# Twelve of the 32 depthwise chunks tap by tap on VectorE, nine rounds of convs on TensorE, the last one the 3x3 conv alone beside the batch norm's chain

## The chip, the cores and the metric

One core of a Trainium2 chip. The time is that of one execution on the device, in microseconds (us); that of a kernel is the median of its runs.

## What is computed

The input x is (8, 32, 64, 64) in float32. A bidirectional LSTM with 16 hidden units runs over the rows, a linear layer brings it back to 32 channels, and with x as a residual it goes into a second block. That block is what the change touches:

```python
def offset_branch(x, dw_w, dw_b, bn_g, bn_b, pw_w, pw_b):
    h = conv2d(x, dw_w, dw_b, padding=1, groups=x.shape[1])   # depthwise 3x3
    h = jax.nn.relu(batchnorm(h, bn_g, bn_b))
    return conv2d(h, pw_w, pw_b, padding=0)                   # 9 offsets a pixel
```

It is computed twice, with the weights of the x and of the y offsets. Beside it stands a full 3x3 conv of the same image from 32 to 32 channels (in the kernel it is already multiplied by the weights that fuse the branches). The offsets then shift the image along x and along y with linear interpolation, both results are projected, and the three are fused, normalized over the batch, passed through ReLU and added to the block's input.

## The kernel before, in words

**Layout.** The 8 images lie as 4 quadrants of 32 channels (128 partitions) by 2 halves `b` of 4096 pixels. All of it is cut into `NCH` = 16 chunks of 8 image rows, 512 pixels (`CH`); chunks 0 to 7 are half 0, chunks 8 to 15 half 1. `pad` is the image with a border of one pixel, 66 x 66. `h_x` and `h_y` take the results of the two depthwise convs (called hx and hy below), `acc` that of the 3x3 conv. `h_y` is stored transposed: within a half, the column index is the slow one (`hyt`, `hy_chunk`).

**Order.** Every engine has its own program, written out by hand; they meet at semaphores. There is no scheduler. An engine does its instructions in the order in which they are written, and one that waits holds all behind it.

**The conv stage** (line 898 on TensorE). Three kinds of jobs, `j` = 0 the 3x3 conv, 1 hx, 2 hy, with 16 chunks each: 48 jobs. Each job is nine taps of four matmuls, one for every quadrant, of 32 x 32 weights over 512 pixels in float32, accumulated in one PSUM bank. Four jobs make a round, and for each tap the matmuls of the four follow one another, so that the 16 positions of 32 x 32 in the array are all in use: quadrant q of job i writes to quadrant (q + i) % 4 of its bank. That makes 12 rounds, on banks 0 to 3 and 4 to 7 in turn (`conv_bank`). A round begins when the banks of the round before last have been read.

A job whose place i is not the usual place of its kind (`PLACES`) lands with its quadrants turned. The conv must be turned back to the image's order; hx and hy can stay turned, if the offset matmuls know the place (`X_PLACE`, `PLACES[2]`).

**Evacuation.** ScalarE (line 466) reads conv and hy banks and adds the bias; a turned bank costs four instructions of 32 partitions in place of one. VectorE (line 670) does that for hx, and takes `bn_stats` of each hx and hy chunk (lines 675 and 679).

**The batch norm's chain** (`norm`, lines 529 to 559). When the last statistics are there VectorE aggregates them, TensorE averages the means over the quadrants (line 786) and then the variances (line 788), ScalarE takes the root (line 401), and VectorE makes scale and shift.

**Offsets.** In four rounds `rd` of four chunks: VectorE (lines 688 and 689) and ScalarE (line 482) apply scale, shift and ReLU to a quarter (2048 elements a partition) of `h_x` and `h_y`; TensorE makes the offsets of x in banks 0 to 3 and of y in banks 4 to 7 (line 921); ScalarE (line 490) and VectorE (line 696) write them in bf16 parts, with masking matmuls between (line 929). After that comes the long loop of the sampling, which is not changed.

**Names the change touches**: `norm_mm` on TensorE, `norm_sqrt`, `relu_y_round` and `parts_x` on ScalarE, `CONV_ROUNDS`, `conv_bank`, `X_PLACE`, `vecs` (a table with one column a vector, loaded at the start).

## Time and profile before

| | us |
|---|---|
| median of 3 runs | 845.68 |
| lowest and highest | 842.84, 846.45 |
| the profiled execution | 846.11 |
| its span, first to last instruction | 844.2 |
| TensorE busy | 729.8 (86%) |
| VectorE busy | 612.0 (73%) |
| ScalarE busy | 492.6 (58%) |
| GpSimd busy | 259.6 (31%) |

All times of the trace count from the span's start. PE is TensorE, PEld its weight loads, DVE VectorE, ACT ScalarE, POOL GpSimd. A float32 matmul leaves two records. An instruction's duration includes its start and its drain, so the next one on the same engine can begin a little before its end. Convs, the norm's chain and offsets lie between 235 and 407 us.

### The profile page before, as it was taken

To read this page: it belongs to the slowest core of one execution; us is meant where nothing else is said; L and a number is where in the kernel's file an instruction comes from. 1 tells how busy PE (TensorE), PEld (TensorE's weight loads), DVE (VectorE), ACT (ScalarE), POOL (GpSimd) and SP (SyncE) were. 2 spreads that over 40 slices of the span, in tenths; PEclk is the share of its full clock that TensorE was granted. 3 is DMA by queue.
4 is the path that set the end of the run, shared out by engine and by line. 5 is a ranking of instruction groups with operands and counts; after the bars stand their busy time and mean duration, and the time that the engine had idled before them with its cause. 6 is when DMAs were issued, how large, how long until landed. Compare 5 with 4: busy or idle time off the path is not lost.

```text
span 844.2 us, 61069 instructions
## 1 busy us (share of the span) xinstructions
PE 729.8 (86%) x27570; PEld 590.9 (70%) x27570; DVE 612.0 (73%) x1126; ACT 492.6 (58%) x1008; POOL 259.6 (31%) x284
## 2 busy tenths in 40 slices
PE   0589999999689999587779999999999999999970
PEld 0355555557258899432469999999989999999960
DVE  4466666665812322568758999999999999999975
ACT  0344444443332432366658888878878887888854
POOL 1122222210000000000224445454465656656533
PEclk9999999999879999789999999999999999999995
DMA  9200000000000000000000000000000000000006
GB/s 238 89 2 2 0 0 0 0 2 1 4 3 4 5 4 4 4 1 1 3 4 0 0 0 0 0 0 0 0 0 0 0 0 0 0 0 0 0 2 199
DMA packets 4062, 12.04 MB, mean 14 GB/s; under 512 B 1391, under 2 KB 1787, under 8 KB 3460
## 3 DMA queue, kind: packets, MB, share of 16 engines
q1 hardware_dynamic: 1716, 4.88, 2.1%
q10 hardware_dynamic: 1522, 4.21, 1.8%
q0 software_dynamic: 768, 2.10, 0.9%
q8 instruction: 48, 0.79, 0.4%
q14 instruction: 8, 0.07, 0.0%
HBM read 6.99 MB, written 4.19 MB: 13 GB/s over the span
## 4 chain that ended last, share of the span: by engine, by line
PE 66%; DVE 17%; ACT 8%; issue 5%; DMA 2%; POOL 2%; ACTq 0%; DVEq 0%; POOLq 0%
PE psum L1022 17%; PE psum L951 16%; PE psum L898 13%; PE psum L977 8%; PE psum L969 5%; DVE wide L608 5%; DVE wide L611 4%; ACT wide L423 4%; ACT wide L419 3%; PE psum L921 2%; DVE offs L696 2%; DMA xs<-in_x_dram 2%; DVE stats L643 1%; POOL out_dram L254 1%; DVE xs L652 1%
## 5 line engine op out<-in xcount | busy, mean ns | idle before, releaser
L509 ACT ACTIVATE wide<-psum 128x512 f32<-128x512 f32 x576 | 301.5, 600 | 15.1 <-PE psum L951 8.1
L951 PE MATMUL psum<-wide,sels 125*32 125x256 bf16 x4608 | 231.9, 275 | 3.1 <-issue 2.5
L1022 PE MATMUL psum<-wide 128*32 128x64 f32 x8192 | 194.9, 220 | 3.4 <-issue 3.4
L720 DVE TENSOR_SCALAR wide<-wide 128x1024 f32<-128x1024 f32 x256 | 180.2, 724 | 2.8 <-ACT wide L509 2.6
L1022 PEld LDWEIGHTS psum<-wide 128*32 128x32 f32 x8192 | 169.6, 110 | 5.2 <-issue 3.9
L727 DVE COPY wide<-psum 128x1024 f32<-128x1024 f32 x128 | 156.1, 1219 | 2.0
L359 POOL COPY wide<-offs 125x256 bf16 (+1 forms) x64 | 28.7, 449 | 389.3 <-DVE offs L696 212.7
L351 POOL TENSOR_SCALAR wide<-wide 128x512 f32<-128x512 f32 x64 | 135.9, 2123 | 7.2 <-ACT wide L509 7.2
L898 PE MATMUL psum<-img,offs 32*32 32x512 f32 x3456 | 112.3, 610 | 5.8 <-ACT img L451 5.8
L977 PE MATMUL psum<-wc,wide 32*64 32x128 f32 x4096 | 112.7, 283 | 1.3 <-issue 1.3
L816 PEld LDWEIGHTS psum<-wide 128*64 128x64 f32 x2048 | 70.3, 137 | 61.0 <-DVE wide L619 60.0
L898 PEld LDWEIGHTS psum<-img,offs 32*32 32x32 f32 x3456 | 95.8, 104 | 21.5 <-issue 8.7
L951 PEld LDWEIGHTS psum<-wide,sels 125*32 125x32 bf16 x4608 | 91.1, 97 | 21.3 <-issue 13.7
L816 PE MATMUL psum<-wide 128*64 128x64 f32 x2048 | 87.2, 228 | 15.0 <-DVE wide L619 13.6
L969 PEld LDWEIGHTS psum<-wc,wide 32*64 32x64 f32 x2048 | 82.0, 133 | 18.3 <-issue 18.1
L969 PE MATMUL psum<-wc,wide 32*64 32x32 f32 x2048 | 89.4, 218 | 4.4 <-POOL wide L364 2.6
L977 PEld LDWEIGHTS psum<-wc,wide 32*64 32x64 f32 x4096 | 91.8, 132 | 1.5 <-issue 1.5
L423 ACT ACTIVATE wide<-wide 128x64 f32<-128x64 f32 x128 | 32.8, 256 | 93.8 <-DVE wide L611 93.8
L804 PE MATMUL psum<-wide 128*64 128x256 f32 x512 | 78.4, 388 | 0.0
L670 DVE TENSOR_SCALAR wide<-psum,vecs 128x512 f32<-128x512 f32 x16 | 11.6, 749 | 76.1 <-PE psum L898 76.1
L619 DVE SCALAR_TENSOR_TENSOR wide<-wide 128x64 f32<-128x64 f32 x128 | 33.2, 259 | 42.3 <-ACT wide L423 42.3
L505 ACT ACTIVATE y<-psum 64x256 f32<-64x256 f32 x64 | 24.2, 379 | 67.5 <-PE psum L969 67.5
(101 smaller groups left out, 772.8 us busy)
## 6 DMA issues: line engine op xcount, KB each, us to landing
xs<-in_x_dram ACTq DMA_DIRECT2D x8, 256.0 KB, 10.7
xs<-in_x_dram SPq DMA_DIRECT2D x8, 256.0 KB, 10.1
out_dram<-wide SPq DMA_DIRECT2D x16, 128.0 KB, 3.5
out_dram<-wide POOLq DMA_DIRECT2D x16, 128.0 KB, 4.2
offs<-in_cw_dram ACTq DMA_DIRECT2D x1, 576.0 KB
sels<-in_sel_dram ACTq DMA_DIRECT2D x1, 562.5 KB
wide<-in_dsc_dram ACTq DMA_DIRECT2D x1, 288.0 KB
offs<-in_dwd_dram ACTq DMA_DIRECT2D x1, 288.0 KB
```

The source lines that it names most:

```text
L351: nc.gpsimd.tensor_scalar(v8[:, par], v8[:, par], 1.0, 1.0, ALU.min, ALU.subtract).then_inc(v8_ready, 1)
L423: nc.scalar.activation(tc_[:, b], cells[:, b, 4, :], ACT.Tanh, scale=0.5).then_inc(tc_ready[b], 1)
L509: nc.scalar.activation(hat_tile(par, i), use_bank(par, hat_use(i)).rearrange("p (q n) -> p q n", q=2), ACT.Abs).then_inc(d_read, 1)
L720: nc.vector.tensor_scalar(v, v, 1.0, 1.0, ALU.min, ALU.subtract).then_inc(v_ready, 1)
L727: nc.vector.tensor_copy(yt[:, par, q:q + 2], psum[:, Y_BANK[q] * CH:(Y_BANK[q] + 2) * CH].rearrange("p (q r m) -> p q r m", q=2, r=HROWS)) ...
L804: last = mm(bank[DQ * d:DQ * d + DQ, (g % 2) * GROUP * S:(g % 2 + 1) * GROUP * S], wx_s[:, d, g, :], xst[:, par, d, :, b * S:(b + 1) * S], ...
L816: last = mm(gates[half, g], whh_s[:, g, half], hst[:, (j - 1) % UNROLL, b * S:(b + 1) * S], start=False, stop=True, skip_group_check=True)
L898: last = mm(conv_bank(m, i)[C * to:C * to + C, :], w, pad[rows, b, r0 + t // 3:r0 + t // 3 + ROWS, t % 3:t % 3 + S], start=(t == 0), stop= ...
L951: last = mm(bank[c, e * SL:(e + 1) * SL], sels[:, k, c], oc[0:NROW, par, :], start=(e == 0), stop=(e == 1))
L969: last = mm(use_bank(par, Y8_USE)[S * e:S * e + S, at:at + C], xc[c, par, r8 * S:(r8 + 1) * S], wcv[c, 0, 8, :], start=(r8 == 0 and tiles ...
L977: last = mm(ps[Y_BANK[q]][S * e:S * e + S, r * P:(r + 1) * P], xc[c, par, r * S:(r + 1) * S], wcv[c, 0, e:8:2, :], start=(r == 0), stop=(r ...
L1022: last = mm(ps[O_BANK][C * q:C * q + C, cols], w, v, start=(group == 0), stop=(group == GROUPS - 1))
```

## The change

**What it does.** VectorE makes twelve depthwise chunks itself, in three blocks of four (`ON_DVE`): hy 0 to 3, hy 4 to 7, hx 0 to 3, all of image half 0. A block of 2048 pixels is nine passes: the first tap times its weight plus the bias (block 0 on VectorE, blocks 1 and 2 on ScalarE), then eight `scalar_tensor_tensor`, each of which multiplies a shifted view of the padded image by a tap's weight and adds it to the block in place. The source of the hy blocks is a transposed view (`rearrange("p h w -> p w h")`). The weights come as 18 new columns of `vecs`. Each block is followed by its own statistics and those of some of TensorE's rounds.

TensorE keeps 36 jobs, nine rounds: eight with both kinds, and a ninth, `CONV_ONLY`, with four chunks of the 3x3 conv. Ahead of its eighth tap stands the matmul of the norm's means, behind it that of the variances; the offset matmuls of round 0 wait for the ninth round's banks one by one.

ScalarE evacuates all of TensorE's banks, hx too. Depthwise chunks always stay turned and cost one instruction; a conv chunk at place 2 costs two of 64 partitions, at places 1 and 3 four of 32. The ninth round's banks are evacuated after the root, after the first ReLU, and between the first two writings of offsets.

The diff, without the lines for constants, semaphores and the weights' layout, and without the split of `norm_mm` into `norm_mean` and `norm_var` (the same two matmuls with the same waits):

```diff
--- before.py
+++ after.py
...
@@ -213,18 +214,36 @@
 
 
 
-        PLACES = {0: 0, 2: 1, 1: 2}
-        TURN = (0, 2, 1)
-        CONV_ROUNDS, made = [], [0, 0, 0]
-        for m in range(3 * NCH // 4):
-            kinds = (0, 2, 1, TURN[m % 3])
-            CONV_ROUNDS.append([])
-            for j in kinds:
-                CONV_ROUNDS[m].append((j, made[j]))
-                made[j] += 1
-        X_PLACE = {n: i for jobs in CONV_ROUNDS for i, (j, n) in enumerate(jobs) if j == 1}
-        def conv_bank(m, i):
-            return ps[4 * (m % 2) + i]
+
+        ON_DVE = ((2, 0), (2, 4), (1, 0))
+        DW_CHUNKS = 4
+        def conv_rounds():
+            conv, hy = iter(range(NCH)), iter(range(NCH // 2, NCH))
+            hx = iter(range(DW_CHUNKS, NCH))
+            rounds = []
+            for m in range(8):
+                rounds.append([(0, 0, next(conv)), (1, 2, next(hy)),
+                               (2, 0, next(conv)) if m % 2 else (2, 1, next(hx)), (3, 1, next(hx))])
+            rounds.append([(i, 0, next(conv)) for i in (0, 2, 1, 3)])
+            return rounds
+        CONV_ROUNDS = conv_rounds()
+        CONV_ONLY = len(CONV_ROUNDS) - 1
+
+        JOB_NO, X_PLACE, Y_PLACE = {}, {n: 0 for n in range(DW_CHUNKS)}, (0, 1)
+        for jobs in CONV_ROUNDS:
+            for i, j, n in jobs:
+                JOB_NO[j, n] = sum(1 for key in JOB_NO if key[0] == j) + 1
+                if j == 1:
+                    X_PLACE[n] = i
+        def conv_bank(m, k):
+            return ps[4 * (m % 2) + k]
+        def dw_block(j, n):
+
+            r0, rows = n * ROWS, DW_CHUNKS * ROWS
+            def src(t):
+                v = pad[:, 0, r0 + t // 3:r0 + t // 3 + rows, t % 3:t % 3 + S]
+                return v if j == 1 else v.rearrange("p h w -> p w h")
+            return src, hxv[:, 0, r0:r0 + rows, :] if j == 1 else hyt[:, 0, :, r0:r0 + rows]
         ROUNDS = 4
         RC = NCH // ROUNDS
 
...
@@ -450,31 +469,38 @@
             act.wait_ge(pad_zero, 2)
             nc.scalar.activation(pad[:, 1, 1:1 + S, 1:1 + S], xv[:, 1], ACT.Identity, bias=coef[:, GN2, 1, 1:2],
                                  scale=coef[:, GN2, 0, 1:2]).then_inc(pad_ready[1], 1)
-            for m, jobs in enumerate(CONV_ROUNDS):
-                for i, (j, n) in enumerate(jobs):
...
-                    act.wait_ge(made_by, n + 1)
-                    if i == PLACES[j]:
-                        last = evacuate(slice(0, P), slice(0, P))
+
+            act.wait_ge(pad_ready[0], 1)
+            for j, n in ON_DVE[1:]:
+                src, to = dw_block(j, n)
+                nc.scalar.activation(to, src(0), ACT.Identity, bias=vecs[:, V_DWB + j - 1:V_DWB + j],
+                                     scale=vecs[:, V_DWW + (j - 1) * K:V_DWW + (j - 1) * K + 1]).then_inc(dw_first, 1)
+
+            def evacuate(m, k):
+                i, j, n = CONV_ROUNDS[m][k]
+                made_by, done = ((conv_mm, conv_ev), (hx_mm, hx_ev), (hy_mm, hy_ev))[j]
+                bias = cbias if j == 0 else vecs[:, V_DWB + j - 1:V_DWB + j]
+                act.wait_ge(made_by, JOB_NO[j, n])
+
+                turns = 0 if j else i
+                for own, at in {0: ((slice(0, P), slice(0, P)),),
+                                2: ((slice(0, S), slice(S, P)), (slice(S, P), slice(0, S)))}.get(
+                                    turns, [(slice(C * q, C * q + C), slice(C * ((q + turns) % Q), C * ((q + turns) % Q) + C))
+                                            for q in range(Q)]):
+                    src = conv_bank(m, k)[at, :]
+                    if j == 2:
+                        to, src = hy_chunk(n, own), src.rearrange("p (h w) -> p w h", h=ROWS)
                     else:
-
-                        for q in range(Q):
-                            at, own = C * ((q + i) % Q), C * ((q + PLACES[j]) % Q)
-                            last = evacuate(slice(own, own + C), slice(at, at + C))
-                    last.then_inc(done, 1)
+                        to = (acc, h_x)[j][own, n * CH:(n + 1) * CH]
+                    last = nc.scalar.activation(to, src, ACT.Identity, bias=bias[at, 0:1])
+                last.then_inc(done, 1)
+
+            for m in range(CONV_ONLY):
+                for k in range(4):
+                    evacuate(m, k)
             norm_sqrt(BN, 2)
+            for k in range(2):
+                evacuate(CONV_ONLY, k)
 
             def relu_y_round(rd):
 
@@ -490,11 +516,14 @@
                         nc.scalar.activation(ob[0][0:ONE_ROW + 1, (RC * rd + 2 * n) * CH:(RC * rd + 2 * n + 2) * CH],
                                              psum[0:ONE_ROW + 1, 2 * n * CH:(2 * n + 2) * CH], ACT.Identity,
                                              bias=vecs[0:ONE_ROW + 1, V_PWB:V_PWB + 1]).then_inc(done, 1)
+                        if rd == 0 and done is part1[0] and n == 0:
+                            evacuate(CONV_ONLY, 3)
                     if done is part1[0] and rd + 1 < ROUNDS:
                         relu_y_round(rd + 1)
 
             act.wait_ge(norm_done, BN + 1)
             relu_y_round(0)
+            evacuate(CONV_ONLY, 2)
             for rd in range(ROUNDS):
                 parts_x(rd)
 
@@ -662,21 +691,32 @@
             nc.vector.tensor_scalar(pad[:, 0, 1:1 + S, 1:1 + S], xv[:, 0], coef[:, GN2, 0, 0:1],
                                     coef[:, GN2, 1, 0:1], ALU.mult, ALU.add).then_inc(pad_ready[0], 1)
 
-            for m, jobs in enumerate(CONV_ROUNDS):
-                for i, (j, n) in enumerate(jobs):
-                    if j == 1:
-                        v = h_x[:, n * CH:(n + 1) * CH]
-                        dve.wait_ge(hx_mm, n + 1)
-                        nc.vector.tensor_scalar(v, conv_bank(m, i)[:, :], vecs[:, V_DWB:V_DWB + 1], None, ALU.add
-                                                ).then_inc(hx_ev, 1)
-                for j, n in jobs:
-                    if j == 2:
-                        dve.wait_ge(hy_ev, n + 1)
-                        last = nc.vector.bn_stats(stats_hy[:, n, :], hy_chunk(n))
-                for j, n in jobs:
-                    if j == 1:
-                        dve.wait_ge(hx_ev, n + 1)
-                        last = nc.vector.bn_stats(stats[:, n, :], h_x[:, n * CH:(n + 1) * CH])
+            def dw_stats(j, n):
+                if j == 1:
+                    return nc.vector.bn_stats(stats[:, n, :], h_x[:, n * CH:(n + 1) * CH])
+                return nc.vector.bn_stats(stats_hy[:, n, :], hy_chunk(n))
+
+            def round_stats(m):
+                for i, j, n in CONV_ROUNDS[m]:
+                    if j:
+                        dve.wait_ge((hx_ev, hy_ev)[j - 1], JOB_NO[j, n])
+                        last = dw_stats(j, n)
+                return last
+
+            for k, (j, n) in enumerate(ON_DVE):
+                src, to = dw_block(j, n)
+                weight = lambda t: vecs[:, V_DWW + (j - 1) * K + t:V_DWW + (j - 1) * K + t + 1]
+                if k == 0:
+                    dve.wait_ge(pad_ready[0], 1)
+                    step(nc.vector.tensor_scalar(to, src(0), weight(0), vecs[:, V_DWB + j - 1:V_DWB + j], ALU.mult, ALU.add))
+                else:
+                    dve.wait_ge(dw_first, k)
+                for t in range(1, K):
+                    step(nc.vector.scalar_tensor_tensor(to, src(t), weight(t), to, ALU.mult, ALU.add))
+                for c in range(DW_CHUNKS):
+                    dw_stats(j, n + c)
+                for m in ((0, 1), (2, 3, 4), (5, 6, 7))[k]:
+                    last = round_stats(m)
             step(last)
             nc.vector.bn_aggr(mv[:, 0, :], stats[:, :, :])
             step(nc.vector.bn_aggr(mv[:, 1, :], stats_hy))
...
@@ -884,25 +933,26 @@
             read = [0, 0, 0]
             for m, jobs in enumerate(CONV_ROUNDS):
                 if m >= 2:
-                    for j, n in CONV_ROUNDS[m - 2]:
-                        read[j] = n + 1
+                    for i, j, n in CONV_ROUNDS[m - 2]:
+                        read[j] = JOB_NO[j, n]
                     pe.wait_ge(conv_ev, read[0])
                     pe.wait_ge(hx_ev, read[1])
                     pe.wait_ge(hy_ev, read[2])
                 for t in range(K):
-                    for i, (j, n) in enumerate(jobs):
+                    if m == CONV_ONLY and t == K - 2:
+                        norm_mean(BN, 2)
+                    for k, (i, j, n) in enumerate(jobs):
                         b, r0 = n // (NCH // 2), n % (NCH // 2) * ROWS
                         for q in range(Q):
                             rows, to = slice(C * q, C * q + C), (q + i) % Q
                             w = cwf[rows, t, rows] if j == 0 else dwd_s[rows, j - 1, t, :]
-                            last = mm(conv_bank(m, i)[C * to:C * to + C, :], w,
+                            last = mm(conv_bank(m, k)[C * to:C * to + C, :], w,
                                       pad[rows, b, r0 + t // 3:r0 + t // 3 + ROWS, t % 3:t % 3 + S],
                                       start=(t == 0), stop=(t == K - 1))
                         if t == K - 1:
                             last.then_inc((conv_mm, hx_mm, hy_mm)[j], 1)
-            norm_mm(BN, 2)
-
-            pe.wait_ge(conv_ev, NCH)
+            norm_var(BN, 2)
+
             pe.wait_ge(dmask_in, 16)
             for rd in range(ROUNDS):
                 b, n0 = rd // 2, rd % 2 * RC
@@ -912,10 +962,13 @@
                     if rd > 0 and n % 2 == 0:
                         for a in range(2):
                             pe.wait_ge(part3[a], 2 * rd - 2 + n // 2 + 1)
+                    if rd == 0 and n != 1:
+
+                        pe.wait_ge(conv_ev, NCH - 2 + max(n - 1, 0))
                     r0 = slice((n0 + n) * ROWS, (n0 + n + 1) * ROWS)
                     for a in range(2):
                         for q in range(Q):
-                            at = (q + (X_PLACE[b * NCH // 2 + n0 + n] if a == 0 else PLACES[2])) % Q
+                            at = (q + (X_PLACE[b * NCH // 2 + n0 + n] if a == 0 else Y_PLACE[b])) % Q
                             rows = slice(C * at, C * at + C)
                             rhs = (hxv if a == 0 else hyt)[rows, b, r0, :]
                             last = mm(ps[RC * a + n][C * q:C * q + C, :], pws[rows, a, :], rhs, start=True, stop=True)
```

**VectorE, between the padding of image half 0 and the batch norm's aggregation.** Before, its first rounds (`wide` holds hx and hy, `img` the padded image):

```order
L662 TENSOR_SCALAR img<-xs,small 128x64x64 [waits pad_zero,norm_done]
L670 TENSOR_SCALAR wide<-psum,vecs 128x512 [waits hx_mm]
L675 BN_STATS offs<-wide 128x6 [waits hy_ev]
L679 BN_STATS stats<-wide 128x6 [waits hx_ev]
L670 TENSOR_SCALAR wide<-psum,vecs 128x512 [waits hx_mm]
L675 BN_STATS offs<-wide 128x6 [waits hy_ev] x2
L679 BN_STATS stats<-wide 128x6 [waits hx_ev]
L670 TENSOR_SCALAR wide<-psum,vecs 128x512 [waits hx_mm] x2
L675 BN_STATS offs<-wide 128x6 [waits hy_ev]
```

Now, its first block, two rounds' statistics and the second block:

```order
L691 TENSOR_SCALAR img<-xs,small 128x64x64 [waits pad_zero,norm_done]
L711 TENSOR_SCALAR wide<-img,vecs 128x64x32 [waits pad_ready0]
L715 SCALAR_TENSOR_TENSOR wide<-img,vecs,wide 128x64x32 [waits link] x8
L697 BN_STATS offs<-wide 128x6 [waits link]
L697 BN_STATS offs<-wide 128x6 x3
L697 BN_STATS offs<-wide 128x6 [waits hy_ev]
L696 BN_STATS stats<-wide 128x6 [waits hx_ev] x2
L697 BN_STATS offs<-wide 128x6 [waits hy_ev]
L696 BN_STATS stats<-wide 128x6 [waits hx_ev]
L715 SCALAR_TENSOR_TENSOR wide<-img,vecs,wide 128x64x32 [waits dw_first]
L715 SCALAR_TENSOR_TENSOR wide<-img,vecs,wide 128x64x32 [waits link] x7
```

The evacuations of hx (line 670) are gone. In front of the first statistics stand nine operations over 2048 elements that wait for nothing of TensorE's.

**TensorE, from its last rounds of convs to the first masking matmul.** Before:

```order
L898 MATMUL psum<-img,offs 32x512 [waits hy_ev,hx_ev,conv_ev]
L898 MATMUL psum<-img,offs 32x512 x143
L786 MATMUL psum<-small,avgs 128x2 [waits mean_in]
L788 MATMUL psum<-small,avgs 128x2 [waits dev_in]
L921 MATMUL psum<-wide,pws 32x512 [waits relu_x,relu_y,dmask_in,conv_ev]
L921 MATMUL psum<-wide,pws 32x512 x31
L929 MATMUL psum<-offs,seq 124x512 [waits part1x]
L929 MATMUL psum<-offs,seq 124x512 [waits part1y]
```

Now:

```order
L949 MATMUL psum<-img,offs 32x512 [waits hy_ev,hx_ev,conv_ev]
L949 MATMUL psum<-img,offs 32x512 x111
L825 MATMUL psum<-small,avgs 128x2 [waits mean_in]
L949 MATMUL psum<-img,offs 32x512 x32
L831 MATMUL psum<-small,avgs 128x2 [waits dev_in]
L974 MATMUL psum<-wide,pws 32x512 [waits relu_y,conv_ev,relu_x,dmask_in]
L974 MATMUL psum<-wide,pws 32x512 x15
L974 MATMUL psum<-wide,pws 32x512 [waits conv_ev]
L974 MATMUL psum<-wide,pws 32x512 x7
L974 MATMUL psum<-wide,pws 32x512 [waits conv_ev]
L974 MATMUL psum<-wide,pws 32x512 x7
L982 MATMUL psum<-offs,seq 124x512 [waits part1x]
```

The matmul of the means (L825) has moved into the last round, ahead of its last 32 matmuls, and the offset matmuls (L974) of the first round wait in three pieces.

**ScalarE, from the root to the second writing of offsets, now** (before, only the root, the ReLU and the writings of offsets stood here):

```order
L420 ACTIVATE small<-small 128x2 [waits sqrt_in]
L495 ACTIVATE seq<-psum,small 128x512 [waits conv_mm]
L495 ACTIVATE seq<-psum,small 64x512 [waits conv_mm]
L495 ACTIVATE seq<-psum,small 64x512
L508 ACTIVATE wide<-wide,small 128x2048 [waits norm_done]
L495 ACTIVATE seq<-psum,small 32x512 [waits conv_mm]
L495 ACTIVATE seq<-psum,small 32x512 x3
L516 ACTIVATE offs<-psum,vecs 124x1024 [waits off_mmx]
L495 ACTIVATE seq<-psum,small 32x512 [waits conv_mm]
L495 ACTIVATE seq<-psum,small 32x512 x3
L516 ACTIVATE offs<-psum,vecs 124x1024 [waits off_mmx]
```

Four evacuations (L495) of conv banks have moved between the root (L420), the ReLU (L508) and the writings of offsets (L516).

## Rows read from the trace of the kernel before

**Rows 1.** Table of stretches: us, then busy us (instructions) by engine, TensorE clock, DMA.
```profile
242.00:348.00 106.00, 105.97 (x3347) 92.64 (x3325) 28.49 (x44) 36.32 (x55) 0.00 (x0) 1.00 0.02 4
348.00:359.30 11.30, 1.18 (x4) 1.00 (x4) 8.96 (x23) 2.99 (x4) 0.00 (x0) 0.59 0.01 3
359.30:363.00 3.70, 3.67 (x44) 1.52 (x53) 0.00 (x0) 0.00 (x0) 0.00 (x0) 0.50 0.00 0
```

**Rows 2.** Waits, 235 to 366 us: who for whom, us, times, longest.
```profile
DVE wide L670 <- PE psum L898: 76.1, 12, 13.7
ACT seq L466 <- PE psum L898: 75.6, 12, 11.3
```

**Rows 3.** Groups by line, 205 to 348 us: busy us, mean ns | idle before.
```profile
L898 PE MATMUL psum<-img,offs 32*32 32x512 f32 x3456 | 112.3, 610 | 5.8 <-ACT img L451 5.8
...
L466 ACT ACTIVATE seq<-psum,small 128x512 f32<-128x512 f32 x12 | 8.2, 687 | 75.6 <-PE psum L898 75.6
L466 ACT ACTIVATE wide<-psum,vecs 128x512 f32<-128x512 f32 x11 | 7.5, 680 | 0.1
```

**Rows 4.** Timeline: padding, then ScalarE's first evacuations of rounds 0, 1, 7, 8, 11.
```profile
231.68 2.42 DVE L662 TENSOR_SCALAR img<-xs,small 128x4096 f32<-128x4096 f32 x1
...
246.83 0.69 ACT L466 ACTIVATE seq<-psum,small 128x512 f32<-128x512 f32 x1 [11.34 <-PE psum L898]
...
248.30 2.75 ACT L466 ACTIVATE seq<-psum,small 32x512 f32<-32x512 f32 x4
256.37 0.69 ACT L466 ACTIVATE seq<-psum,small 128x512 f32<-128x512 f32 x1 [5.32 <-PE psum L898]
...
311.12 0.69 ACT L466 ACTIVATE seq<-psum,small 128x512 f32<-128x512 f32 x1 [5.34 <-PE psum L898]
...
320.00 0.69 ACT L466 ACTIVATE seq<-psum,small 128x512 f32<-128x512 f32 x1 [4.84 <-PE psum L898]
...
347.43 0.69 ACT L466 ACTIVATE seq<-psum,small 128x512 f32<-128x512 f32 x1 [5.13 <-PE psum L898]
```

**Rows 5.** Timeline of VectorE after the last round of convs.
```profile
349.81 1.27 DVE L679 BATCH_NORM_STATS2 stats<-wide 128x6 f32<-128x512 f32 x2
351.12 0.59 DVE L681 BATCH_NORM_AGGREGATE small<-stats 128x2 f32<-128x96 f32 x1
...
356.47 1.35 DVE L688 TENSOR_SCALAR wide<-wide,small 128x2048 f32<-128x2048 f32 x1
357.85 1.23 DVE L689 TENSOR_SCALAR wide<-wide 128x2048 f32<-128x2048 f32 x1
```

**Rows 6.** Timeline of TensorE and ScalarE in the norm's chain and the first offsets.
```profile
352.41 0.59 PE L786 MATMUL psum<-small,avgs 128*128 128x2 f32 x2 [4.43 <-DVE small L536]
353.83 0.59 PE L788 MATMUL psum<-small,avgs 128*128 128x2 f32 x2 [0.84 <-DVE small L541]
359.33 5.83 PE L921 MATMUL psum<-wide,pws 32*32 32x512 f32 x64 [4.91 <-DVE wide L689]
...
356.47 2.10 ACT L482 ACTIVATE wide<-wide,small 128x2048 f32<-128x2048 f32 x1 [1.61 <-DVE small L557]
363.03 1.11 ACT L490 ACTIVATE offs<-psum,vecs 124x1024 bf16<-124x1024 f32 x1 [4.47 <-PE psum L921]
```

**Rows 7.** Groups of VectorE by form, whole span: durations by size.
```profile
L608 DVE SCALAR_TENSOR_TENSOR wide<-wide 128x128 f32<-128x128 f32 x128 | 40.2, 314 | 17.4 <-ACT wide L419 12.7
...
L775 DVE TENSOR_TENSOR wide<-wide,xs 128x1024 f32<-128x1024 f32 x8 | 9.2, 1218 | 1.4 <-ACT wide L515 1.4
L688 DVE TENSOR_SCALAR wide<-wide,small 128x2048 f32<-128x2048 f32 x4 | 5.4, 1339 | 0.0
...
L539 DVE TENSOR_TENSOR small<-small 128x2 f32<-128x2 f32 x3 | 0.5, 160 | 0.1
```

**Rows 8.** GpSimd's copy of image rows: 400 to 590 us (x), 630 to 830 us (y).
```profile
L364 POOL COPY wide<-img 128x256 f32 x27 | 14.9, 552 | 6.5 <-ACT wide L509 6.5
...
L364 POOL COPY wide<-img 128x256 f32 x29 | 26.9, 928 | 4.1 <-ACT wide L509 3.6
```

More of the change, by code:

```diff
@@ L45 @@
 V_DWB, V_BNG, V_BNB, V_PWB = 6, 8, 10, 12
-NVEC = 14
+V_DWW = 14
+NVEC = V_DWW + 2 * K
 def build(nc, x, wx, whh, wlin, gate_bias, gate_ind, cw, fus, dsc, dwd, pw, dm, vec, avg, sel, pos, out):
@@ L452, in _ @@
                                  scale=coef[:, GN2, 0, 1:2]).then_inc(pad_ready[1], 1)
-            for m, jobs in enumerate(CONV_ROUNDS):
-                for i, (j, n) in enumerate(jobs):
-                    if j == 1:
-                        continue
-                    made_by, done = (conv_mm, conv_ev) if j == 0 else (hy_mm, hy_ev)
-                    bias = cbias if j == 0 else vecs[:, V_DWB + 1:V_DWB + 2]
-                    def evacuate(own, at):
-                        src = conv_bank(m, i)[at, :]
-                        if j == 2:
-                            to, src = hy_chunk(n, own), src.rearrange("p (h w) -> p w h", h=ROWS)
-                        else:
-                            to = acc[own, n * CH:(n + 1) * CH]
-                        return nc.scalar.activation(to, src, ACT.Identity, bias=bias[at, 0:1])
-                    act.wait_ge(made_by, n + 1)
-                    if i == PLACES[j]:
-                        last = evacuate(slice(0, P), slice(0, P))
-                    else:
-                        for q in range(Q):
-                            at, own = C * ((q + i) % Q), C * ((q + PLACES[j]) % Q)
-                            last = evacuate(slice(own, own + C), slice(at, at + C))
-                    last.then_inc(done, 1)
@@ L780, in _, with norm_mean, norm_var @@
             mm = nc.tensor.matmul
-            def norm_mm(i, n):
-                m = avgs[:, 0 if i <= GN2 else 1, :]
-                pe.wait_ge(mean_in, i + 1)
-                mm(ps[NORM_BANK][:, 0:n], m, nt[:, 0, 0:n], start=True, stop=True).then_inc(mean_out, 1)
-                pe.wait_ge(dev_in, i + 1)
-                mm(ps[NORM_BANK][:, 8:8 + n], m, nt[:, 1, 0:n], start=True, stop=True).then_inc(var_out, 1)
+            def norm_mean(i, n):
+                pe.wait_ge(mean_in, i + 1)
+                mm(ps[NORM_BANK][:, 0:n], avgs[:, 0 if i <= GN2 else 1, :], nt[:, 0, 0:n], start=True, stop=True
+                   ).then_inc(mean_out, 1)
+            def norm_var(i, n):
+                pe.wait_ge(dev_in, i + 1)
+                mm(ps[NORM_BANK][:, 8:8 + n], avgs[:, 0 if i <= GN2 else 1, :], nt[:, 1, 0:n], start=True, stop=True
+                   ).then_inc(var_out, 1)
+            def norm_mm(i, n):
+                norm_mean(i, n)
+                norm_var(i, n)
             pe.wait_ge(misc_in, 32)
```

5 lines of the change are left out of this document (2 added, 3 removed).

## The prediction, made before the result was known

> **What bounds the kernel now.** I began with the table of stretches, because the change touches one stage only: from the moment the padded image is ready (235.6 us) to the first offset matmuls (359.3 us). [Rows 1] show TensorE busy for 105.97 of the 106.00 us from 242 to 348, at a granted clock of 1.00; so the convs are bound by TensorE. The list of waits says the same from the other side: VectorE stood 76.1 us and ScalarE 75.6 us waiting for these matmuls [rows 2]. In the list by line the convs are 3456 records (two per matmul, 1728 matmuls in 12 rounds), 112.3 us [rows 3]. The timeline of ScalarE gives the pitch: the first evacuation of round 0 starts at 246.83, of round 7 at 311.12, of round 8 at 320.00, of round 11 at 347.43 [rows 4]. That is (347.43 - 246.83) / 11 = 9.15 us a round; round 0 took 11.2 us, from 235.6, before and after alike.
>
> Behind the convs comes a chain in which TensorE is nearly idle (1.18 of 11.30 us [rows 1]): last statistics, aggregation, two small matmuls, root, the normalization's factors, then ReLU over 2048 elements [rows 5, 6]. VectorE has its last statistics done at 351.08, the matmul of the means starts at 352.41, that of the variances at 353.83, the offset matmuls at 359.33, the masking ones at about 365.09 (359.33 + 5.83 less the pipelining). I call this last moment M; all later work hangs on it and is not touched.
>
> **TensorE's part.** The change takes 12 of 48 jobs away, 3 of 12 rounds. Each of the four jobs of a round still has a place of its own, so I keep the pitch. Round 8 is then the last: its first job is done where round 8's is now, 320.00; the other three need 0.54 us more, as at the end of round 11 (347.43, then idle from about 347.97). The matmul of the means goes in ahead of its eighth tap; it costs the 0.59 us of its row [rows 6]. The variance matmul starts at 320.00 + 0.54 + 0.6 = 321.15 instead of 353.83, if VectorE has handed over in time. **Gain so far: 32.7 us.** Of this 27.4 is three rounds; the other 5.3 is the chain's first half, now under round 8.
>
> **VectorE's part.** Image half 0 is padded at 231.68 + 2.42 = 234.10 [rows 4]. Then come, in three blocks of four chunks (2048 elements): one first tap as tensor_scalar (the ReLU's first operation has this form and size, 1.34 us [rows 7]), 24 scalar_tensor_tensor, 32 bn_stats at a pitch of 0.61 us (two in 1.27 [rows 5]). The trace has no scalar_tensor_tensor of 2048. The add of 1024 takes 1218 ns, small operations of two elements 160: 1.035 ns an element, so 2278 ns for 2048; the scalar_tensor_tensor of 128 elements takes 314 where that line gives 290, so 24 more [rows 7]. I take 2.30 us, and a pitch of 2.34 with the wait on the link semaphore (the ReLU's second operation, which waits likewise, starts 0.03 us after the first one's end [rows 5]). Eight are 18.7 us, four statistics 2.4.
>
> Walk it: block 0 ends at 234.10 + 1.4 + 18.7 + 2.4 = 256.6. Statistics of rounds 0 and 1: the last chunk of round 1 is evacuated at about 259.7 (256.37 for its first job [rows 4], then 0.6 + 0.6 + 1.4 + 0.7), so 260.3. Block 1 to 281.4, rounds 2 to 4 to 286.8. Block 2 to 307.9, rounds 5 and 6 to 311.0. Round 7's last chunk is evacuated at 311.12 + 0.6 + 0.6 + 1.4 + 0.7 = 314.4, its statistics end at 315.05. The aggregates and the copy add 1.3 (351.08 to the 352.41 of the matmul): 316.3. TensorE wants it before its eighth tap, 7/9 of 9.1 us into round 8, at about 318.3. So VectorE has some 2 us to spare behind round 7, and more for what lies before it: all 24 operations could grow by 0.2 us each before TensorE is held.
>
> ScalarE takes over the four hx evacuations' work that VectorE did, and two first taps of about 2.1 us (its ReLU of 2048 [rows 6]) before 247, when it now idles for 11 us. A round costs it 2.7 or 3.3 us of 9.15: hidden. The wider vecs load is hidden too: it lands behind megabytes of image on the same queue; bound 0 to 0.1 us. If that cover were gone, the extra 9 KB would be less than that.
>
> **The tail, where something is given back.** After the variance matmul the chain is the same, 5.5 us to the offset matmuls (353.83 to 359.33): 326.65. ScalarE squeezes the evacuations of round 8's first two jobs (0.7 + 1.4) between root and ReLU: 321.15 + 1.05 + 2.0 = 324.2 against norm_done at 323.75, so its ReLU ends at 326.3, still with VectorE's two operations (321.15 + 5.25 = 326.4). Free. The third job's four pieces (2.75 us, the four in [rows 4]) end at 329.05, under the first half of the offset matmuls. The fourth is queued on ScalarE behind the first evacuation of offsets, and TensorE's last quarter of the round waits for it. If the clock falls as it does now ([rows 1]: 0.50 from 359.3 to 363), the first half lasts 3.7 us (359.33 to the 363.03 of [rows 6]), to 330.35; offsets 1.0, four pieces 2.7: 334.1; last quarter 0.9 to 1.8: **M at 335.0 to 335.9**, for 365.09 now. If the idle 4.9 us don't cost the clock, 328.5, but ScalarE is only free at 329.05: M at 333.7. Gain 29.2 to 31.4; I take 30, nearer the cold end, since [rows 1] show 0.59 over a gap of 11.3 us, which is about 2 us at full clock before it fell. What was a 32.7 us gain gives 2 to 3 us back to ScalarE's queue.
>
> The profiled execution took 846.11 us, 0.43 over the median of the runs (845.68), so the difference is small: 846.1 - 30 = **816 us**. With the clock's phase in this and the next three rounds, 812 to 820. No change that is smaller than 0.5% can be told from none here.
>
> **What the sum rests on: strides.** Two of the three blocks are hy, and read the image with an inner step of 66 elements (264 bytes), 32 at a time. No VectorE row has such a read from SBUF. From below, the price is nothing: ScalarE's evacuation of hy reads PSUM with an inner step of 64 elements and takes 680 ns against 687 for the plain one [rows 3]. From above, the nearest is GpSimd's copy of image rows, 552 ns on average in the x pass and 928 in the y pass, which steps the same way [rows 8]: 1.68 times. I take nothing for VectorE, as ScalarE is the nearer kind of engine and one operand in three is strided, and keep the other.
>
> The Trainium skill (Advanced Engine Details and Errata, section SBUF Cachelines) says that an engine needs at least two hits on a 16-byte line to hide the access; by it a float32 step of 264 bytes would be slowed. It gives no factor. No VectorE row here shows it; what it would come to at one more cycle an element is rival 2.
>
> **Rivals.**
> 1. *Strided taps as slow as on GpSimd.* Streaming is 2048 x 1.035 = 2.12 us of an operation; 16 hy operations grow by 0.68 x 2.12 = 1.44 us each, 23.1 in all. VectorE becomes the bound: its work without waits is 1.4 + 24 x 2.34 + 32 x 0.61 = 77.1 us, from 234.1 to 311.2; so 334.3, and the means out at 335.6. TensorE, held before its eighth tap, goes cold: 64 matmuls of two taps at twice 1.0 us each, so variance 4.75 us after the means, offsets at +10.2, M at +18.7 = 354.3: 10.8 us gained, **835**. Chance 0.10.
> 2. *Strided taps at half rate.* Each streams twice as long: 2.12 us more for each of 16 and 0.9 for the first tap, 34.8 in all: means at 347.3, M at 366.0: **847**, no change. The trace neither shows nor excludes it. Chance 0.13.
> 3. *Slower than before: two float32 sources in SBUF at half rate.* All 24 taps cost 4.42 instead of 2.30: 50.9 us more, means at 363.4, M at 382.1: **863**. It decides from about 4.4 us an operation on; below 2.5 nothing is held at all. Against it: with 2.07 ns an element the operation of 128 would take 160 + 265 = 425 ns and the add of 1024 2.3 us, where they take 314 and 1218 [rows 7]. Chance 0.03. The Trainium skill (Vector Engine (DVE) Microarchitecture Reference, section Points that are easy to get wrong) states that this instruction with two non-bf16 SBUF sources halves throughput. By that rule the time is 863; the row of 128 speaks against it.
> 4. *The round's pitch or the tail a little worse* (waits of TensorE on evacuations, VectorE and TensorE reading one image): between 820 and 835. Chance 0.05. *Better than 812*: 0.03.
>
> That the change doesn't do what it says is out: its order of instructions has 1296 matmuls of the conv line and 24 scalar_tensor_tensor of 2048.
>
> **How the numbers follow.** Forecast 0.66, rivals 0.10, 0.13, 0.03, 0.05 and 0.03. The range 811 to 840 holds the forecast, rival 1 and most of 4: 0.82. Faster by over 0.5% (under 841.5): 0.66 + 0.10 + 0.05 + 0.03 = 0.84. Rival 2 lies within 0.5% for the most part: 0.11. Slower (over 849.9): rival 3 and 2's upper end, 0.05.
>
> **What would show it.** A scalar_tensor_tensor of 2.3 us in both shapes, hy and hx; nine rounds at 9.1 us without a hold before the eighth tap; TensorE's idle time between variance and offset matmuls about 5 us; one wait of some 3 us before the last quarter of the first offset round. The forecast is wrong if the hy shape takes over 2.5 us, if TensorE waits for the means, or if the pitch of the rounds has grown.

## The result, and the profile after

The changed kernel takes **843.69 us** (median of 12 runs, 841.83 to 846.23), the kernel before in the same series 846.52 (12 runs). The ratio is 0.9968, 95% interval 0.9953 to 0.9983: 0.3% faster. The interval leaves out 1, but the gain is less than the 0.5% that the prediction called distinguishable. I had forecast 816 and a range of 811 to 840. The profiled execution took 842.90 us, its span 841.1.

The groups by line between 234 and 345 us (busy us, mean ns, idle time before), kernel after:

```profile
L715 DVE SCALAR_TENSOR_TENSOR wide<-img,vecs,wide 128x2048 f32<-128x2048 f32 x24 | 84.5, 3520 | 0.8
L696 DVE BATCH_NORM_STATS2 stats<-wide 128x6 f32<-128x512 f32 x16 | 10.3, 677 | 0.0
L697 DVE BATCH_NORM_STATS2 offs<-wide 128x6 f32<-128x512 f32 x16 | 10.2, 679 | 0.1
```

and VectorE's timeline, kernel after (start, us, engine, line, operation, count, idle before):

```profile
234.71 2.23 DVE L711 TENSOR_SCALAR wide<-img,vecs 128x2048 f32<-128x2048 f32 x1
236.97 33.12 DVE L715 SCALAR_TENSOR_TENSOR wide<-img,vecs,wide 128x2048 f32<-128x2048 f32 x8
270.13 3.07 DVE L697 BATCH_NORM_STATS2 offs<-wide 128x6 f32<-128x512 f32 x5
...
275.49 33.06 DVE L715 SCALAR_TENSOR_TENSOR wide<-img,vecs,wide 128x2048 f32<-128x2048 f32 x8
...
315.71 19.05 DVE L715 SCALAR_TENSOR_TENSOR wide<-img,vecs,wide 128x2048 f32<-128x2048 f32 x8
...
340.74 0.68 DVE L696 BATCH_NORM_STATS2 stats<-wide 128x6 f32<-128x512 f32 x1
```

The mean of 3520 ns in the first table hides two kinds: eight taps of the third block, hx, take 19.05 us (2.34 each, the forecast's 2.30), the sixteen of the hy blocks 33.1 us for eight, about 4.10 each. From one start to the next it is 2.39 us in hx and 4.14 in hy. The last statistics end at 341.42 us, where I had 315.05.

TensorE's timeline, kernel after, answers to [rows 6]:

```profile
236.22 82.08 PE L949 MATMUL psum<-img,offs 32*32 32x512 f32 x2528 [5.82 <-ACT img L470]
342.74 0.59 PE L825 MATMUL psum<-small,avgs 128*128 128x2 f32 x2 [24.44 <-DVE small L565]
343.26 4.08 PE L949 MATMUL psum<-img,offs 32*32 32x512 f32 x64
347.27 0.59 PE L831 MATMUL psum<-small,avgs 128*128 128x2 f32 x2
352.65 6.66 PE L974 MATMUL psum<-wide,pws 32*32 32x512 f32 x48 [4.79 <-DVE wide L729]
360.75 1.92 PE L974 MATMUL psum<-wide,pws 32*32 32x512 f32 x16 [1.44 <-ACT seq L495]
362.59 1.29 PE L982 MATMUL psum<-offs,seq 124*124 124x512 bf16 x5
```

TensorE did its part: it stood before the eighth tap of the ninth round at 318.30, as forecast. Then it waited 24.44 us for the means. The stretches of the same profile (PE, PEld, DVE, ACT, POOL busy, clock, DMA) show what that did to its clock:

```profile
236.00:318.00 82.00, 81.78 (x2528) 67.43 (x2528) 81.40 (x39) 29.34 (x39) 0.00 (x0) 0.98 0.02 4
318.00:342.70 24.70, 0.30 (x7) 0.00 (x0) 24.33 (x22) 0.00 (x0) 0.00 (x0) 0.56 0.00 0
342.70:347.90 5.20, 5.12 (x68) 2.03 (x68) 0.65 (x5) 0.00 (x0) 0.00 (x0) 0.50 0.01 3
```

At 0.50 (1.2 GHz) the remaining two taps took 4.08 us. M, the start of the masking matmuls, is at 362.59; in the kernel before it was at about 365.09. Up to 318 both engines are busy (VectorE 81.40, TensorE 81.78 of 82.00 us); in the next 24.70 us VectorE works for 24.33 and TensorE for 0.30. So a stage that TensorE bound became one that VectorE bounds, at almost the same length.

### The profile page after: what moved, and what is told of

Same layout as the page of the kernel before. It is cut to its first block, busy times and chain, and to the rows that moved or that the text cites. A ratio compares the mean times of both kernels' runs of the same rounds, so it can differ in the third digit from the quotient of the medians.

```text
span 841.1 us, 59340 instructions
## 1 busy us (share of the span) xinstructions
PE 709.1 (84%) x26706; PEld 563.9 (67%) x26706; DVE 687.2 (82%) x1135; ACT 492.1 (59%) x1001; POOL 260.0 (31%) x284
## 4 chain that ended last, share of the span: by engine, by line
PE 54%; DVE 29%; ACT 8%; issue 4%; DMA 2%; POOL 2%; ACTq 0%; DVEq 0%; POOLq 0%
PE psum L1075 17%; PE psum L1004 16%; DVE wide L715 10%; PE psum L1030 8%; DVE wide L637 5%; PE psum L1022 5%; DVE wide L640 4%; ACT wide L442 4%; ACT wide L438 3%; PE psum L974 2%; DMA xs<-in_x_dram 2%; DVE offs L736 2%; DVE offs L697 1%; DVE stats L696 1%; DVE stats L672 1%
## 5 line engine op out<-in xcount | busy, mean ns | idle before, releaser
L949 PE MATMUL psum<-img,offs 32*32 32x512 f32 x2592 | 86.2, 617 | 5.8 <-ACT img L470 5.8
L715 DVE SCALAR_TENSOR_TENSOR wide<-img,vecs,wide 128x2048 f32<-128x2048 f32 x24 | 84.5, 3520 | 0.8
L949 PEld LDWEIGHTS psum<-img,offs 32*32 32x32 f32 x2592 | 68.5, 104 | 21.0 <-issue 9.3
L648 DVE SCALAR_TENSOR_TENSOR wide<-wide 128x64 f32<-128x64 f32 x128 | 33.1, 259 | 42.3 <-ACT wide L442 42.3
```

The costliest lines, as they stand in the source:

```text
L715: step(nc.vector.scalar_tensor_tensor(to, src(t), weight(t), to, ALU.mult, ALU.add))
L949: last = mm(conv_bank(m, k)[C * to:C * to + C, :], w, pad[rows, b, r0 + t // 3:r0 + t // 3 + ROWS, t % 3:t % 3 + S], start=(t == 0), stop= ...
```

## Experiments

The open question after the result: what makes the sixteen hy taps slow. The trace alone does not say that it is the stride. The slow blocks ran beside a busy TensorE that read the same image, and the fast one beside a TensorE idle for all but its first 2.6 us. The hy blocks also write another pattern (32 elements, then a jump). One row speaks against the first doubt already: the strided first tap started at 234.71 and took 2.23 us, for 1.35 where the source is contiguous (hx12, below), and TensorE began only at 236.22, when a tap of 1.35 us would have been over.

### hx12: twelve hx chunks on VectorE, none of hy

```diff
-        ON_DVE = ((2, 0), (2, 4), (1, 0))
+        ON_DVE = ((1, 0), (1, 4), (1, 8))
...
-                rounds.append([(0, 0, next(conv)), (1, 2, next(hy)),
-                               (2, 0, next(conv)) if m % 2 else (2, 1, next(hx)), (3, 1, next(hx))])
+                rounds.append([(0, 0, next(conv)), (1, 2, next(hy)),
+                               (2, 0, next(conv)) if m % 2 else (2, 1, next(hx)), (3, 2, next(hy))])
...
-        JOB_NO, X_PLACE, Y_PLACE = {}, {n: 0 for n in range(DW_CHUNKS)}, (0, 1)
+        JOB_NO, X_PLACE, Y_PLACE = {}, {n: 0 for n in range(3 * DW_CHUNKS)}, (1, 1)
...
-                turns = 0 if j else i
+                turns = i if j == 0 else i - 1 if j == 2 else 0
```

(and `dw_block` takes its half of the image from n, with one more wait on `pad_ready[1]` on both engines.) hy has to have one place in a whole half, since the transposed store mixes its chunks in each offset matmul; so the hy of place 3 is turned to place 1 in two instructions.

> VectorE's twelve chunks are all hx (0 to 11), read along image rows; TensorE keeps all 16 hy. Stride theory (an inner step of 264 bytes halves VectorE's rate): all 24 taps last 2.34 us, the means are out before TensorE wants them, the masking matmuls start at about 335.5, time 816 +-4 us. Rival, contention (the taps are slow because TensorE reads the same image at the time; the fast hx block of the changed kernel ran beside an idle TensorE for all but its first 2.5 us): the taps that run beside the convs still last about 4.1 us, VectorE ends later still than in the changed kernel and the time is 843 to 850 us.

Measured: **815.34 us** (4 runs), ratio 0.9642 (0.9613 to 0.9672). VectorE's timeline in hx12:

```profile
235.60 19.06 DVE L717 SCALAR_TENSOR_TENSOR wide<-img,vecs,wide 128x2048 f32<-128x2048 f32 x8
...
261.32 19.05 DVE L717 SCALAR_TENSOR_TENSOR wide<-img,vecs,wide 128x2048 f32<-128x2048 f32 x8
...
287.61 19.05 DVE L717 SCALAR_TENSOR_TENSOR wide<-img,vecs,wide 128x2048 f32<-128x2048 f32 x8
...
312.67 0.69 DVE L698 BATCH_NORM_STATS2 offs<-wide 128x6 f32<-128x512 f32 x1 [0.54 <-ACT wide L496]
315.48 0.69 DVE L698 BATCH_NORM_STATS2 offs<-wide 128x6 f32<-128x512 f32 x1 [2.11 <-ACT wide L496]
```

All three blocks ran beside the convs, all at 2.34 us a tap. So TensorE's reading of the image does not by itself make a tap slow. The last statistics end at 316.17, the means wait for TensorE (matmul at 318.98), not the other way round.

### hy_rows: the changed kernel, hy blocks read along rows

```diff
-                return v if j == 1 else v.rearrange("p h w -> p w h")
+                return v if j == 1 else pad[:, 0, t // 3:t // 3 + S, r0 + t % 3:r0 + t % 3 + rows]
```

> As the changed kernel, but the two hy blocks read the image along rows instead of columns (same count, same destination, same place in the program; hy chunks 0 to 7 hold other pixels' sums, so the output is not the reference's). Stride theory: 16 taps fall from 4.10 to 2.34 us, VectorE hands over at about 315 to 318, time 816 +-4 us. Rival, contention with TensorE: taps stay at 4.1 us beside the convs, time 843 us. Rival, the destination's pattern (32 elements, then a jump) is what costs: stays at 4.1 us, 843 us.

Measured: 817.92 us (4 runs), ratio 0.9668 (0.9638 to 0.9697). The taps by their source line (shortest, median and longest in ns, then the first and last start):

```profile
L715 DVE SCALAR_TENSOR_TENSOR wide<-img,vecs,wide x24: 2333/2352/2354, 235.8 to 303.7; 128x2048 f32<-128x2048 f32 x24
```

Destination, place, count and neighbours are those of the changed kernel; the source's step alone has changed (and with it which pixels are summed: these hy chunks hold other pixels' sums). That settles the cause. The 2.6 us over hx12 come up again in same_tiles.

### steps: how far a source may step

A series ahead of the blocks, each operation behind the last one's end, on 1024 float32 elements; F is the image as one row, X and Y contiguous scratch:

```diff
+            for s in (1, 2, 3, 4, 5, 8):
+                stt(Y[:, 0:N], F[:, 0:N * s:s], X[:, 0:N])
+            stt(Y[:, 0:N].rearrange("p (a c) -> p a c", c=2), F[:, 0:4 * N].rearrange("p (a c) -> p a c", c=8)[:, :, 0:2],
+                X[:, 0:N].rearrange("p (a c) -> p a c", c=2))
+            stt(X[:, 0:N], F[:, 0:N], Y[:, 0:4 * N:4])
+            stt(Y[:, 0:4 * N:4], F[:, 0:N], X[:, 0:N])
+            stt(Y[:, 0:4 * N:4], F[:, 0:4 * N:4], Y[:, 0:4 * N:4])
+            for a, b in ((1, 1), (4, 1), (1, 4)):
+                step(nc.vector.tensor_scalar(Y[:, 0:N * b:b], F[:, 0:N * a:a], 0.5, 0.0, ALU.mult, ALU.add))
...
-                for t in range(1, K):
+                for t in range(1, K if k == 2 else 2):
```

> A series on VectorE ahead of the blocks, 1024 float32 elements each: scalar_tensor_tensor with the source at step 1, 2, 3, 4, 5, 8, then pairs (2 of every 8), then only in1 at step 4, only the output at step 4, all three at step 4; then tensor_scalar plain, source at step 4, output at step 4. The two hy blocks have one tap each instead of eight, so hy chunks 0 to 7 are not the reference's. Theory, two hits in 16 bytes suffice: 1.24 us at steps 1, 2 and for pairs, about 2.2 from step 4 on, step 3 between; tensor_scalar 0.7 plain and 1.2 to 1.3 at step 4. Rival, any step but 1 halves: 2.2 from step 2 on. Rival, only steps over 64 bytes or so cost: 1.24 throughout.

One run; its time (820.09 us) is compared with nothing. VectorE's timeline in steps; a line with x2 is two operations. In the first such line the second operation has its own line below; the second holds the two strided tensor_scalar:

```profile
248.41 1.28 DVE L712 SCALAR_TENSOR_TENSOR wide<-img,vecs,wide 128x1024 f32<-128x1024 f32 x1
249.73 1.33 DVE L712 SCALAR_TENSOR_TENSOR wide<-img,vecs,wide 128x1024 f32<-128x1024 f32 x1
251.09 4.08 DVE L712 SCALAR_TENSOR_TENSOR wide<-img,vecs,wide 128x1024 f32<-128x1024 f32 x2
252.91 2.26 DVE L712 SCALAR_TENSOR_TENSOR wide<-img,vecs,wide 128x1024 f32<-128x1024 f32 x1
255.21 2.14 DVE L712 SCALAR_TENSOR_TENSOR wide<-img,vecs,wide 128x1024 f32<-128x1024 f32 x1
257.38 2.12 DVE L712 SCALAR_TENSOR_TENSOR wide<-img,vecs,wide 128x1024 f32<-128x1024 f32 x1
259.54 1.29 DVE L712 SCALAR_TENSOR_TENSOR wide<-img,vecs,wide 128x1024 f32<-128x1024 f32 x1
260.86 2.18 DVE L712 SCALAR_TENSOR_TENSOR wide<-img,vecs,wide 128x1024 f32<-128x1024 f32 x1
263.07 2.23 DVE L712 SCALAR_TENSOR_TENSOR wide<-img,vecs,wide 128x1024 f32<-128x1024 f32 x1
265.34 2.40 DVE L712 SCALAR_TENSOR_TENSOR wide<-img,vecs,wide 128x1024 f32<-128x1024 f32 x1
...
267.77 0.69 DVE L726 TENSOR_SCALAR wide<-img 128x1024 f32<-128x1024 f32 x1
268.50 2.48 DVE L726 TENSOR_SCALAR wide<-img 128x1024 f32<-128x1024 f32 x2
```

In the order of the code: step 1 1.28 us, step 2 1.33, step 3 1.78 (the 4.08 of two, less the 2.26 of the second and a gap of 0.04), step 4 2.26, step 5 2.14, step 8 2.12. Pairs out of every eight elements: 1.29. A strided in1 costs 2.18, a strided output 2.23, all three together 2.40, so the prices do not add up. tensor_scalar goes from 0.69 to 1.22 us ((2.48 - 0.04) / 2) with either side at step 4. The full price is there from 16 bytes on, it does not grow with the step, and two neighbours in 16 bytes avoid it. The Trainium skill (Advanced Engine Details and Errata, section SBUF Cachelines) says that an engine needs at least two hits on a 16-byte line to hide the access, without a factor; these rows agree with it and add one. An operation on float32 takes 1.65 to 1.8 times as long (2.26 or 2.12 for 1.28, 1.22 for 0.69, and 4.10 for 2.35 in the taps), with a strided output as well.

### means_last: what the hold before the eighth tap cost

```diff
-                    if m == CONV_ONLY and t == K - 2:
-                        norm_mean(BN, 2)
...
-            norm_var(BN, 2)
+            norm_mm(BN, 2)
```

> The changed kernel with the means' matmul behind the ninth round again, so that VectorE's late statistics do not hold TensorE before its eighth tap. My theory: two taps of the ninth round ran at 1.2 GHz behind the means, 4.0 us between the two small matmuls' chain; without that the variance matmul follows 1.4 us behind the means' instead of 4.5, and the time falls by 3 us, to about 840.5 us. Rival (TensorE's hold costs nothing, as the clock is lost either way and the offsets' rounds set the time): 843.5 us.

Measured: 840.16 us (9 runs), ratio 0.9941 (0.9916 to 0.9967), against 0.9968 (0.9953 to 0.9983) for the changed kernel in its own series. By the ratios that is 0.0027 or some 2.3 us less, and the intervals overlap, so the times alone do not show it; the medians, 3.5 us apart, stand in different series. TensorE's timeline in means_last shows the mechanism itself:

```profile
343.28 0.58 PE L825 MATMUL psum<-small,avgs 128*128 128x2 f32 x2 [22.44 <-DVE small L565]
344.70 0.59 PE L831 MATMUL psum<-small,avgs 128*128 128x2 f32 x2 [0.84 <-DVE small L570]
350.08 8.10 PE L972 MATMUL psum<-wide,pws 32*32 32x512 f32 x48 [4.79 <-DVE wide L729]
```

From the means' matmul to the variances' it is 1.42 us, for 4.53. But the first 48 records of offsets last 8.10 us for 6.66: the mean granted clock is 0.65 over these records and 0.80 over those of the changed kernel. Of the 3.1 us the masking matmuls keep 1.8: from the convs' start to M it is 361.28 - 236.72 = 124.6 us, against 362.59 - 236.22 = 126.4. The first matmul of the sampling (406.17 for 407.41) keeps 1.7. So the hold cost some 1.8 us by the traces; the rest of the difference in time is not located.

### conv_first: what the round beside the chain is worth, once VectorE is in time

hx12 with the round of the 3x3 conv alone moved to the front:

```diff
-            rounds.append([(i, 0, next(conv)) for i in (0, 2, 1, 3)])
-            return rounds
+            return [[(i, 0, next(conv)) for i in (0, 2, 1, 3)]] + rounds
...
-            for m in range(CONV_ONLY):
+            for m in range(CONV_ONLY + 1):
...
-                for m in ((0, 1), (2, 3, 4), (5, 6, 7))[k]:
+                for m in ((1, 2), (3, 4, 5), (6, 7, 8))[k]:
```

(all evacuations behind the root gone, both small matmuls behind the last round, `wait_ge(conv_ev, NCH)` as before.)

> hx12 with the round of the 3x3 conv alone as the first round, both small matmuls behind the last one, and all banks evacuated in order; so nothing of TensorE's lies beside the norm's chain. By my steps: last statistics at 320.6 + 3.3 + 0.7 = 324.6, means 325.9, masking matmuls 12.8 us behind (as in the kernel before) at 338.7 for 336.2 in hx12: 2.5 us slower, 818 us. Rival (hiding the round is worth the whole chain's first half, 5.3 us): 820.5 us. Rival (it is worth nothing, as ScalarE's evacuations give it back): 815.3 us.

Measured: 818.89 us (6 runs), ratio 0.9676 (0.9642 to 0.9709); hx12 in the same rounds (label hx12_again) 814.19 us, ratio 0.9616 (0.9590 to 0.9641).

> hx12 unchanged, to stand on the same chip and in the same rounds as the next three: 815.3 us, ratio 0.964 to the kernel before.

The round is worth something: "nothing" is out. Whether it is my 2.5 us or the rival's 5.3, the medians (4.7 apart, with conv_first's runs from 813.6 to 822.6) don't tell. In the two profiled executions the masking matmuls start at 338.83 and 337.12, the convs at 236.35 and 236.63: 2.0 us apart, and the spans are 816.4 and 814.2 us. Both are nearer my 2.5.

### hx12_evac: VectorE takes the last turned bank

```diff
-                        if rd == 0 and done is part1[0] and n == 0:
-                            evacuate(CONV_ONLY, 3)
...
             relu_round(0)
+            dve.wait_ge(conv_mm, NCH)
+            i, j, n = CONV_ROUNDS[CONV_ONLY][3]
+            for q in range(Q):
+                at = C * ((q + i) % Q)
+                last = nc.vector.tensor_scalar(acc[C * q:C * q + C, n * CH:(n + 1) * CH], conv_bank(CONV_ONLY, 3)[at:at + C, :],
+                                               cbias[at:at + C, 0:1], None, ALU.add)
+            last.then_inc(last_ev, 1)
```

> hx12, but the fourth bank of the ninth round is evacuated by VectorE (four tensor_scalar of 32 partitions, about 3 us, behind its first two ReLU operations), where it now idles 3.8 us, instead of by ScalarE behind the first writing of offsets. Theory (ScalarE's queue is what holds the last quarter of the first offset round, 3.1 us in hx12): TensorE goes on without the wait, masking matmuls start 3 to 4 us earlier, 811 to 812 us. Rival (TensorE at its low clock is what sets this stretch, or VectorE now hands its offsets over later): within 1 us of hx12.

Measured: 812.25 us (6 runs), ratio 0.9595 (0.9571 to 0.9620), beside hx12's 814.19: 1.9 us lower, with intervals that overlap. First offset round of hx12_again, TensorE's timeline:

```profile
327.61 4.47 PE L976 MATMUL psum<-wide,pws 32*32 32x512 f32 x48 [4.79 <-DVE wide L731]
335.23 1.96 PE L976 MATMUL psum<-wide,pws 32*32 32x512 f32 x16 [3.14 <-ACT seq L496]
337.12 3.67 PE L984 MATMUL psum<-offs,seq 124*124 124x512 bf16 x8
```

and of hx12_evac:

```profile
327.74 5.30 PE L982 MATMUL psum<-wide,pws 32*32 32x512 f32 x64 [4.79 <-DVE wide L730]
332.97 1.08 PE L990 MATMUL psum<-offs,seq 124*124 124x512 bf16 x4
```

The wait of 3.14 us is gone and M comes 4.15 us earlier, as expected. The next round of offsets starts at 341.40 for 344.84 and the first matmul of the sampling at 376.72 for 380.14, so 3.4 us are kept up to there. Why the medians are only 1.9 us apart the runs don't show; the profiled execution of hx12_again is the slowest of its five. It is the fastest version of this study, by its median 34 us below the kernel before.

### same_tiles: x and y offsets in the same tiles

hy_rows and the changed kernel have one more thing in common: in their first offset round 48 records take 6.95 and 6.66 us, in hx12 4.41, although the mean granted clock over them is higher (0.76 and 0.80 for 0.63). There x and y chunks both lie at place 0, in hx12 at 0 and 1. Chunks at one place use the same four tiles (positions of 32 x 32) of TensorE's array. This run is hx12 with hy at place 0 as well:

```diff
-                rounds.append([(0, 0, next(conv)), (1, 2, next(hy)),
-                               (2, 0, next(conv)) if m % 2 else (2, 1, next(hx)), (3, 2, next(hy))])
+                rounds.append([(0, 2, next(hy)), (2, 2, next(hy)),
+                               (3, 1, next(hx)) if m % 2 else (3, 0, next(conv)), (1, 0, next(conv))])
...
-        JOB_NO, X_PLACE, Y_PLACE = {}, {n: 0 for n in range(3 * DW_CHUNKS)}, (1, 1)
+        JOB_NO, X_PLACE, Y_PLACE = {}, {n: 0 for n in range(3 * DW_CHUNKS)}, (0, 0)
```

> hx12 with hy turned back to place 0, so that x and y chunks of the offset matmuls stand in the same quadrants and use the same four tiles of TensorE's array in rounds 0 to 2 (in the changed kernel that is so in round 0; in the kernel before x and y always differ). Theory: x and y matmuls then take turns in the same tiles instead of running side by side; the first 48 records go from 4.4 to about 6.8 us, as they last in the changed kernel (6.66), and each of rounds 1 and 2 loses 2 us or more: 818 to 822 us. Rival (the 6.66 us were the clock's phase): 815.3 us.

Measured: 823.86 us (6 runs), ratio 0.9748 (0.9714 to 0.9783), 9.7 us above hx12 (814.19 in the same rounds) and 2 above the expected range. TensorE's timeline, offset rounds 0 to 3:

```profile
327.65 7.00 PE L977 MATMUL psum<-wide,pws 32*32 32x512 f32 x48 [4.79 <-DVE wide L731]
...
345.60 7.07 PE L977 MATMUL psum<-wide,pws 32*32 32x512 f32 x64 [0.42 <-DVE offs L738]
...
360.43 7.69 PE L977 MATMUL psum<-wide,pws 32*32 32x512 f32 x64
...
375.73 3.67 PE L977 MATMUL psum<-wide,pws 32*32 32x512 f32 x64 [0.42 <-DVE offs L738]
```

and rounds 1 and 2 of hx12_again:

```profile
344.84 3.67 PE L976 MATMUL psum<-wide,pws 32*32 32x512 f32 x64 [0.42 <-DVE offs L738]
...
356.29 4.65 PE L976 MATMUL psum<-wide,pws 32*32 32x512 f32 x64
```

Rounds 1 and 2 have both kinds at place 0 and last 7.07 and 7.69 us; round 3, where hx is at place 3, lasts 3.67. In hx12_again rounds 1 and 2 last 3.67 and 4.65. The clock is not the reason: in round 1 it is granted in full (1.00) in both. So matmuls of different tiles run side by side here, those of the same tiles one after another. Nor do the convs' changed places matter: the means' matmul starts at 319.88 and 319.85. At the first matmul of the sampling (386.71 for 380.14) 6.6 us are lost; where the rest of the 9.7 goes is open.

## Why the prediction was wrong

**What held.** The pitch of TensorE's rounds: nine rounds, TensorE ready for the means at 318.3. A tap of 2.30 us where the source is contiguous (2.34 to 2.35 measured); the statistics' pitch; ScalarE's two first taps hidden. The tail: in hx12 the variance matmul starts at 321.57 (forecast 321.15), the offset matmuls at 326.75 (326.65), the last quarter waits 3.13 us for ScalarE, and M is at 336.18 (335.0 to 335.9). With contiguous taps the sum of 816 us comes out as 815.34 in hx12 and as 817.92 in hy_rows, which keeps everything else of the change.

**The step that failed.** "I take nothing for VectorE, as ScalarE is the nearer kind of engine": the price of the strided source. It was 1.75 us a tap (4.14 for 2.39 from start to start), 28 us for sixteen, and 0.9 for the first tap (2.23 for the 1.35 of hx12). By it VectorE handed over the means at 342.7 us, not before the 318.3 at which TensorE wanted them. Compared with hx12 the means' matmul comes 23.8 us later (342.74 for 318.98), the variances' 25.7, as the two taps between them ran at half the clock, and M 26.4: that is the miss. My reason read ScalarE's evacuation from PSUM [rows 3] as evidence for an operation on SBUF. It is the memory that differs, and not the engine: in the kernel before, VectorE too reads PSUM at a step of 64 elements for nothing (line 738, 421 ns in the x pass, which reads plainly, and 417 in the y pass). The second reason, one strided operand in three, does not help either: in steps one costs 2.26, 2.18 or 2.23 us, all three 2.40. The row that did step through SBUF, GpSimd's [rows 8] with its 1.68, was at hand; by it the time would have been 835. ScalarE, too, pays on SBUF: its two first taps in the changed kernel, hy then hx, took 4.29 and 2.12 us (in hx12, both hx, 4.08 together).

**The rival that came nearest** is the second, half rate, with a chance of 0.13: 847 us and M at 366.0, for 843.7 and 362.6. The strided taps are what it names, but they don't fall to half rate: its price (2.12 us a tap more) was too dear by almost 0.4. The measured 1.75 lies midway between it and the 1.44 of rival 1, whose 835 us were too low by 9. The range ended at 840 and left this case out. The third, two float32 sources at half rate, is refuted: 24 taps of 2.34 us in hx12 have two. The Trainium skill (Vector Engine (DVE) Microarchitecture Reference, section Points that are easy to get wrong) states that rule; no run here agrees with it.

**What I had not counted**: the change puts x and y in the same tiles for the first offset round. `X_PLACE` and `Y_PLACE` stand in the change, and my sum has no term for them. In the changed kernel the first 48 records of offsets take 6.66 us for the 4.41 of hx12. Little of that reaches M, because the last quarter then waits less for ScalarE (1.44 us for 3.13): from the convs' start to M hy_rows needs 0.7 us more than hx12 (337.08 - 235.91 for 336.18 - 235.72). The rest of its 2.6 us lies in offset rounds 1 and 2 (4.83 and 5.09 us for 3.67 and 4.59), where x and y stand in different tiles and the granted clock is lower (0.74 and 0.71 for 1.00 and 0.79).
